# Self-attention in two transformer layers: the side steps of a head placed in steps 0 to 5 of its eight

## The chip, the core and the metric

The kernel runs on one core of a Trainium2 chip. The metric is the device time in microseconds (us) of one launch. The core has a matrix engine (TensorE, PE in the profile, with its weight loads as PEld), a vector engine (VectorE, DVE), an activation engine (ScalarE, ACT), GpSimd (POOL) and SyncE (SP), which here only issues DMAs. Each engine runs its own instruction list in order, and the lists meet at semaphores only.

## What is computed

Two sequences of 1024 tokens by 256 go through two layers, one after the other, which makes four rounds (sequence by layer). Each layer is self-attention, cross-attention to 77 context rows of 192, and a gated feed-forward part:

```python
x = x + attention(layer_norm(x, g1, b1), layer_norm(x, g1, b1), wq1, wk1, wv1, wo1, bo1)
x = x + attention(layer_norm(x, g2, b2), context, wq2, wk2, wv2, wo2, bo2)
x = x + geglu_ff(layer_norm(x, g3, b3), w_ff1, b_ff1, w_ff2, b_ff2)
```

Attention has 16 heads of 64: `q = x @ wq`, `k = ctx @ wk`, `v = ctx @ wv`, softmax of `q k^T / 8`, times v, times `wo`. Everything is float32 in the reference. The kernel splits a float32 operand into a high and a low float16 part and multiplies three times (high by high, high by low, low by high).

## The kernel before

The change touches the self-attention of each round only. There the 16 heads go in 8 pairs, a pair has two head units (head 0, then head 1), and a unit has eight steps, 0 to 7. One step of a head makes a 128x1024 tile of scores. Per step the program holds:

- **peaks**: two matmuls (L769) of single precision parts for the unit that comes next, each into one of two PSUM banks, and for each a `tensor_reduce` on DVE (L1299, "minima") that finds the row maxima. PE may write the bank again when DVE has read it. After the last peak of the next unit (step 6), DVE combines them (L1303), and at the start of step 7 PE transposes the result (L776, "shift"), DVE copies it (L1309), and SP moves it by DMA into a row of `qb`, which the first score of the next unit needs (L796).
- **score**: four matmuls (L789, L796), then two exponentials on ACT (L1120, L1121), one to float32 and one to float16.
- **low part**: the difference of the two, one step later: in steps 1, 3, 5 and 7 ("refine", of tiles 0, 2, 4 and 6) on DVE (L1314), in the others ("polish", tiles 1, 3, 5 and, in step 0 of the next unit, 7) on POOL (L636).
- **value**: 24 short matmuls (L814 to L818) for the tile of three steps ago. After tiles 3 and 7 DVE scales the sum ("gather", L1320 and L1322).
- **one side step or none**, on PE right in front of the score: q, k or v of the next pair (half of the tokens each, L688 to L690; q and k have 6 matmuls of 512 columns, v has 24 of 128), a merge (four transposes of the finished output of the pair before, L826), or a context part (ck, cm, cv: key, key times query weights, and value of the cross-attention). All use one PSUM bank, `work1`. ACT copies the high part out, in front of the exponentials of its step; DVE then takes the low part out ("take", placed between its two minima of that step), and only then may PE begin the next side step. The takes are L1258 (q, k), L1264 (v), L1270 (merge), L1274 (ck, two instructions), L1280 (cm), L1289 (cv, three instructions).
- **weights**: SP fetches them, POOL scales and splits them in three instructions ("split": L585, L586, L589). In head 0 the split W of a 128x1024 piece stands in step 3 (pairs 0 to 5). In head 1 the split S (next q, k, v weights, 128x768) stands in step 3 and the split C (context weights) in step 7. The split S waits until PE has finished every side step placed up to there, its own step 3 included.

In POOL's list the order is polish 7 (of the unit before), polish 1, the split of step 3, polish 3, polish 5, the split of step 7. A table of numbers in `self_unit` says which step a side step goes into; each engine walks the same list of steps and issues its own share of each.

Of the kernel before, what the change touches and what calls it, by code (L numbers as in the profile page):

```python
# [115 lines left out]
Step = collections.namedtuple("Step", "kind step par head ahead")  # L116
# [6 lines left out]
def take(step):  # L123

    return Step("take", (step.kind, step.step), step.par, step.head, step.ahead)
# [12 lines left out]
def queries(par, ahead):  # L138
    return [Step("q", b, par, 0, ahead) for b in range(BLKS)]


def key_blocks(par, ahead):
    return [Step("k", b, par, 0, ahead) for b in range(BLKS)]


def values(par, ahead):
    return [Step("v", b, par, 0, ahead) for b in range(2)]


def maxima(par, head):  # L150

    first = [Step("arrive", 0, par, 0, 0)] if head == 0 else []
    tiles = [[Step("max", (t, h), par, head, 0) for h in range(BLKS)] for t in range(TILES)]
    tiles[0] = first + tiles[0]
    tiles[-1] = tiles[-1] + [Step("combine", 0, par, head, 0)]
    return tiles


def low(s, par, head):

    return [Step("polish" if s in POLISHED else "refine", s, par, head, 0)]


def value(s, par, head):

    out = [Step("value", s, par, head, 0)]
    if s % KEY_STEPS == KEY_STEPS - 1:
        out.append(Step("gather", s // KEY_STEPS, par, head, 0))
    return out


def self_unit(pair, head):

    par, last, first = pair % 2, pair == PAIRS - 1, pair == 0
    nxt, behind = (((par, 1), (1 - par, 0)), ((1 - par, 0), (1 - par, 1)))[head]
    prv = (par, 0) if head == 1 else (1 - par, 1)
    before = head == 1 or not first
    after = (1 - head) if last else 2
    peaks_of = maxima(*nxt)[1:] if after else [[]] * (TILES - 1)
    peaks_of.append(maxima(*behind)[0] if after > 1 else [])  # L180
    placed = collections.defaultdict(list)
    if not last and head == 0:
        placed[0] = [Step("start", 0, 1 - par, 0, 1)]
        for at, step in zip((0, 1, 2, 4), queries(1 - par, 1) + key_blocks(1 - par, 1)):
            placed[at].append(step)
    elif not last:
        for at, step in zip((1, 3), values(1 - par, 1)):
            placed[at].append(step)
    if head == 1 and not first:
        for at, h in ((4, 0), (6, 1)):  # L190
            placed[at].append(Step("merge", h, 1 - par, 0, -1))
    if head == 0:
        placed[5].append(Step("ck", 0, par, 0, 0))
        placed[7].append(Step("cm", 0, par, 0, 0))
    else:
        placed[5].append(Step("cv", 0, par, 0, 0))
    loads = collections.defaultdict(list)
    if head == 0:
        if pair + 2 <= PAIRS:
            loads[1].append(Step("fetch", ("S", pair + 2), par, 0, 0))  # L200
        if pair < 6:
            loads[3].append(Step("split", ("W", pair), par, 0, 0))
        loads[6].append(Step("fetch", ("C", pair + 1), par, 0, 0))
    else:
        if pair + 2 <= PAIRS:
            loads[3].append(Step("split", ("S", pair + 2), par, 0, 0))
        loads[7].append(Step("split", ("C", pair + 1), par, 0, 0))
        if pair < 5:
            loads[7].append(Step("fetch", ("W", pair + 1), par, 0, 0))
    out = [Step("unit", 0, par, head, 0)]  # L210
    for s in range(TILES):
        peaks = [step for step in peaks_of[s] if step.kind == "max"]
        if s == TILES - 1 and after:
            out.append(Step("shift", 0, *nxt, 0))
        out += [step for step in peaks_of[s] if step.kind == "arrive"] + peaks[:1]
        out += placed[s]
        out.append(Step("score", s, par, head, 0))
        out += [take(step) for step in placed[s] if step.kind in HIGH]
        out += peaks[1:] + [step for step in peaks_of[s] if step.kind == "combine"]
        out += loads[s]  # L220
        if s >= 1:
            out += low(s - 1, par, head)
        elif before:
            out += low(TILES - 1, *prv)
        if s >= LAG:
            out += value(s - LAG, par, head)
        elif before:
            out += value(TILES - LAG + s, *prv)
    return out


def self_steps():

    out = [Step("start", 0, 0, 0, 0)]
    out += taken(queries(0, 0) + key_blocks(0, 0) + values(0, 0))
    out += [Step("split", ("S", 1), 0, 0, 0)]
    out += sum(maxima(0, 0), []) + [Step("shift", 0, 0, 0, 0)] + maxima(0, 1)[0]
    for pair in range(PAIRS):
        out += self_unit(pair, 0) + self_unit(pair, 1)
    par = (PAIRS - 1) % 2  # L240
    out += low(TILES - 1, par, 1)
    for s in range(TILES - LAG, TILES):
        out += value(s, par, 1)
    return out + taken([Step("merge", h, par, 0, 0) for h in range(BLKS)])
# [1338 lines left out]
```

How the kernel before makes its waits and increments, by code:

```python
        def hold(eng, sem_, value):  # L444
            eng.wait_ge(sem_, value)
            eng.sem_inc(held, 1)
# [10 lines left out]
            def fetch(g, kind, n):  # L458
                i, l = fetched[0], g % LAYERS
                fetched[0] += 1
                e = i % 2
                if kind == "W":
                    dest, source = raw[e][:, :], io["pieces"][l * PIECES + n, :, :]
                else:
                    dest, source = raw[e][:, 0:6 * P], io["pairs"][(2 * l + (kind == "C")) * PAIRS + n, :, :]
                if i >= 2:
                    sp.wait_ge(raw_used[e], i // 2)
                sp.dma_start(dest, source).then_inc(raw_loaded[e], 16)
# [4 lines left out]
                def spread(which, step):  # L474
                    hold(sp, a.work_free, pace.n("take") + 1 + HIGH_RING)
                    if step.ahead:
                        sp.wait_ge(a.scores_full, pace.pairs(2 * TILES) + (CREDIT - 4 * TILES))
                    for head in range(2):
                        mine, others = [slice(r, r + DH) for r in (head * DH, (1 - head) * DH)]
                        up, low = [part[mine, :] for part in staged["qk".index(which)]]
# [8 lines left out]
                def do(step, pair):  # L491
# [10 lines left out]
                    elif step.kind == "shift":  # L502
                        sp.wait_ge(a.peak_free, pace.n(*PEAK) + 1 + PEAK_RING)
                        row = DH if step.head == 0 else 0
# [339 lines left out]
            def turn(index, p):  # L845
                pe.wait_ge(norm_ready, index * TILES + 2 * (p + 1))
                if p >= 2:
```

## Time and profile before

| what | value |
|---|---|
| three runs | 2564.97 us median (2563.12 to 2571.7) |
| the profiled execution | 2564.95 us |
| its span, first to last instruction | 2563.2 us |
| self-attention of round 1, pairs 0 to 7 | about 57 to 427 us of the span |
| one pair, shift to shift | 45.55 us |
| a side step's share of PE: q or k, v, merge, cm, ck, cv | 1.3, 1.34, 0.43, 0.4, 0.2, 0.73 us |

PE, DVE and ACT run side by side, so a share of busy time does not say which of them sets the pace; the lists of waits and the order of time around one wait do. The pattern of a pair repeats through a round within hundredths of a microsecond, so one pair in the middle (pair 3 of round 1, its head 1 from 217 to 240 us) stands for the rest. Ends of matmuls are modelled; distances between starts are not, and a PE wait is best read from them: behind the second peak matmul of a step, with the 24 value matmuls in between, the next item starts 0.96 us later if nothing holds it.

### The profile page before, as it was taken

How to read it: one execution, taken by the hardware profiler on the slowest of the kernel's cores; microseconds unless marked ns; L12 is line 12 of the kernel's file. 1: busy time of each engine (PE TensorE's matmuls, PEld its weight loads, DVE VectorE, ACT ScalarE, POOL GpSimd, SP SyncE). 2: the span in 40 equal slices, each digit the busy share in tenths (PEclk: the TensorE clock that was granted, in tenths of full speed). 3: DMA queues.
4: the chain of work that ended last, by engine and by line, in shares of the span. 5: the costliest groups of instructions: out<-in, count | busy, mean ns of one | idle time of the engine just before them, and what ended most of it. 6: DMA issues, size and time to landing. Idle time of an engine off the chain costs nothing.

```text
span 2563.2 us, 59118 instructions
## 1 busy us (share of the span) xinstructions
PE 2234.4 (87%) x25392; PEld 1483.4 (58%) x25392; DVE 1760.3 (69%) x3148; ACT 1475.6 (58%) x1948; POOL 1165.7 (45%) x730
## 2 busy tenths in 40 slices
PE   4999998879699999878959999988797999998788
PEld 1566666565366666656525666665653666666565
DVE  6888884545588888454548888845456888885454
ACT  2887885324288888432327888853243888884232
POOL 3667663212176666321216666632122676652311
PEclk8999999889799999888969999999897999999889
DMA  3312210000131221000023122100002223110000
GB/s 80 84 47 73 65 45 18 9 9 15 32 84 47 76 63 45 18 9 10 15 64 79 52 69 70 45 18 9 10 15 49 66 55 84 47 33 18 18 1 17
DMA packets 52437, 106.62 MB, mean 42 GB/s; under 512 B 9552, under 2 KB 13648, under 8 KB 52176
## 3 DMA queue, kind: packets, MB, share of 16 engines
q1 hardware_dynamic: 52176, 102.84, 15.1%
q8 instruction: 200, 3.28, 0.5%
q14 instruction: 61, 0.50, 0.1%
HBM read 50.25 MB, written 2.10 MB: 20 GB/s over the span
## 4 chain that ended last, share of the span: by engine, by line
PE 62%; DVE 19%; ACT 11%; issue 4%; DMA 2%; POOL 1%; SPq 1%; POOLq 0%; DVEq 0%; ACTq 0%
PE scores L688 7%; PE scores L689 7%; PE scores L690 7%; PE work L769 6%; PE scores L796 6%; PE scores L789 6%; DVE minima L1299 6%; DVE prob L1314 3%; PE work L688 3%; PE work L690 3%; PE work L689 3%; ACT prob L1120 3%; PE work L818 3%; PE work L814 3%; PE work L816 3%
## 5 line engine op out<-in xcount | busy, mean ns | idle before, releaser
L636 POOL TENSOR_TENSOR prob<-prob 128x1024 f16<-128x1024 f32 x256 | 582.5, 2275 | 557.1 <-ACT prob L1121 546.4
L1299 DVE TENSOR_REDUCE minima<-work 128x1 f32<-128x512 f32 x1024 | 681.3, 683 | 52.5 <-PE work L769 36.2
L1120 ACT ACTIVATE prob<-scores 128x1024 f32<-128x1024 f32 x512 | 526.0, 1027 | 125.9 <-PE scores L796 109.1
L1121 ACT ACTIVATE prob<-scores 128x1024 f16<-128x1024 f32 x512 | 522.9, 1021 | 0.0
L814 PE MATMUL work<-vals,prob 128*128 128x65 f16 x4096 | 429.7, 193 | 15.4 <-POOL prob L636 13.3
L818 PE MATMUL work<-vals,prob 128*128 128x65 f16 x4096 | 430.3, 195 | 0.0
L816 PE MATMUL work<-vals,prob 128*128 128x64 f16 x4096 | 430.2, 193 | 0.0
L814 PEld LDWEIGHTS work<-vals,prob 128*128 128x128 f16 x4096 | 383.5, 99 | 77.9 <-POOL prob L636 15.1
L769 PE MATMUL work<-ka,qa 128*128 128x512 f16 x1024 | 401.8, 396 | 24.9 <-DMA kb<-staged_k 15.7
L816 PEld LDWEIGHTS work<-vals,prob 128*128 128x128 f16 x4096 | 380.5, 97 | 58.1
L818 PEld LDWEIGHTS work<-vals,prob 128*128 128x128 f16 x4096 | 381.0, 97 | 0.0
L1314 DVE TENSOR_TENSOR prob<-prob 128x1024 f16<-128x1024 f32 x256 | 340.9, 1332 | 18.6 <-ACT prob L1121 17.6
L789 PE MATMUL scores<-qa,ka 128*128 128x512 f16 x1024 | 306.3, 381 | 6.3 <-DVE staged_q L1258 6.0
L796 PE MATMUL scores<-qb,kb 128*128 128x512 f16 (+1 forms) x1024 | 306.6, 381 | 2.7 <-DMA qb<-shift_rows 2.5
L688 PE MATMUL scores<-wide,oT 128*128 128x256 f16 x768 | 213.6, 278 | 12.8 <-DVE prob L1496 7.1
L605 POOL TENSOR_TENSOR var_eps<-mean_var,eps 128x2 f32<-128x2 f32 x48 | 11.3, 236 | 464.7 <-DVE mean_var L1333 464.3
L689 PE MATMUL scores<-wide,oT 128*128 128x256 f16 x768 | 213.5, 278 | 0.0
L690 PE MATMUL scores<-wide,oT 128*128 128x256 f16 x768 | 213.2, 278 | 0.0
L1135 ACT ACTIVATE hT<-work,params 128x256 f16<-128x256 f32 x96 | 54.4, 566 | 233.3 <-PE work L852 220.1
L688 PE MATMUL scores<-hT,wide 128*128 128x512 f16 (+1 forms) x416 | 172.4, 414 | 4.5 <-DVE prob L1496 4.5
L796 PEld LDWEIGHTS scores<-qb,kb 128*128 128x128 f16 (+1 forms) x1024 | 99.9, 98 | 127.6 <-DMA qb<-shift_rows 8.4
L769 PEld LDWEIGHTS work<-ka,qa 128*128 128x128 f16 x1024 | 100.3, 98 | 125.8 <-DVE minima L1299 42.9
(166 smaller groups left out, 4593.4 us busy)
## 6 DMA issues: line engine op xcount, KB each, us to landing
qa<-staged_q SPq DMA_DIRECT2D x128, 128.0 KB, 2.4
ka<-staged_k SPq DMA_DIRECT2D x128, 128.0 KB, 2.4
raw_even<-in_pairs SPq DMA_DIRECT2D x32, 384.0 KB, 3.4
raw_odd<-in_pairs SPq DMA_DIRECT2D x32, 384.0 KB, 3.3
raw_odd<-in_pieces SPq DMA_DIRECT2D x20, 512.0 KB, 3.5
raw_even<-in_pieces SPq DMA_DIRECT2D x20, 512.0 KB, 3.7
qb<-staged_q SPq DMA_DIRECT2D x64, 128.0 KB, 2.4
kb<-staged_k SPq DMA_DIRECT2D x64, 128.0 KB, 2.4
```

Of the source, the lines that this page charges most:

```text
L636: pool.tensor_tensor(prob[1][:, slot, :], prob32[:, slot, :], prob[0][:, slot, :], ALU.subtract).then_inc(a.polished, 1)
L688: pe.matmul(out, left[0], right[0], start=first, stop=False)
L689: pe.matmul(out, left[0], right[1], start=False, stop=False)
L690: return pe.matmul(out, left[1], right[0], start=False, stop=last)
L769: pe.matmul(out[:, :], qa[par][head][:, t * P:(t + 1) * P], ka[par][head][:, h * BLK:(h + 1) * BLK], start=True, stop=True)\
L796: last = pe.matmul(out[:, at], kb[par][head][rows_, keys], qb[par][head][rows_, q], start=False, stop=True)
L814: pe.matmul(out, p_hi, v[:, DH:VW], start=(first and i == 0 and t == 0), stop=False, skip_group_check=True)
L816: pe.matmul(out[:, 0:DH], p_hi, v[:, 0:DH], start=False, stop=False, skip_group_check=True)
L818: last = pe.matmul(out, p_lo, v[:, DH:VW], start=False, stop=(k == TILES - 1), skip_group_check=True)
L1120: act.activation(prob32[:, n % RING, :], source, ACT.Exp)
L1121: act.activation(prob[0][:, n % RING, :], source, ACT.Exp)\
L1299: dve.tensor_reduce(minima[:, t, h:h + 1], out[:, :], AX.X, ALU.max, negate=True)\
```

## The change

Only the numbers in `self_unit` differ; two of the changed places, and the whole as a table:

```diff
     if head == 1 and not first:
-        for at, h in ((4, 0), (6, 1)):
+        for at, h in ((3, 0), (4, 1)):
             placed[at].append(Step("merge", h, 1 - par, 0, -1))
     if head == 0:
-        placed[5].append(Step("ck", 0, par, 0, 0))
-        placed[7].append(Step("cm", 0, par, 0, 0))
+        placed[4].append(Step("ck", 0, par, 0, 0))
+        placed[5].append(Step("cm", 0, par, 0, 0))
```

| step | 0 | 1 | 2 | 3 | 4 | 5 | 6 | 7 |
|---|---|---|---|---|---|---|---|---|
| head 0 before | q0 | q1 | k0 | - | k1 | ck | - | cm |
| head 0 now | q0 | q1 | k0 | k1 | ck | cm | - | - |
| head 1 before | - | v0 | - | v1 | m0 | cv | m1 | - |
| head 1 now | v0 | - | v1 | m0 | m1 | cv | - | - |

Pair 0 has no merges; pair 7 has no q, k and v. POOL's and SP's lists keep every row in its place; on PE, ACT and DVE a side step's rows move with its step. DVE's list in head 1 of a pair with merges, from the take of v1 on (`vals` is the v take, `oT` a merge take, `prob` a refine, `xv` the cv take, `minima` the maxima of one peak). Before:

```order
L1264 SCALAR_TENSOR_TENSOR vals<-work,vals 128x8x64
L1299 TENSOR_REDUCE minima<-work 128x1
L1314 TENSOR_TENSOR prob<-prob 128x1024
L1299 TENSOR_REDUCE minima<-work 128x1
L1270 TENSOR_TENSOR oT<-work,oT 128x512
L1299 TENSOR_REDUCE minima<-work 128x1 x2
L1289 SCALAR_TENSOR_TENSOR xv<-work,mask,xv 124x64 x3
L1299 TENSOR_REDUCE minima<-work 128x1
L1314 TENSOR_TENSOR prob<-prob 128x1024
L1299 TENSOR_REDUCE minima<-work 128x1
L1270 TENSOR_TENSOR oT<-work,oT 128x512
L1299 TENSOR_REDUCE minima<-work 128x1
```

And now:

```order
L1264 SCALAR_TENSOR_TENSOR vals<-work,vals 128x8x64
L1299 TENSOR_REDUCE minima<-work 128x1
L1320 RECIPROCAL inv<-work 128x4
L1322 TENSOR_TENSOR o_nat<-work,inv 128x4x64
L1299 TENSOR_REDUCE minima<-work 128x1
L1270 TENSOR_TENSOR oT<-work,oT 128x512
L1299 TENSOR_REDUCE minima<-work 128x1
L1314 TENSOR_TENSOR prob<-prob 128x1024
L1299 TENSOR_REDUCE minima<-work 128x1
L1270 TENSOR_TENSOR oT<-work,oT 128x512
L1299 TENSOR_REDUCE minima<-work 128x1 x2
L1289 SCALAR_TENSOR_TENSOR xv<-work,mask,xv 124x64 x3
```

The v1 take is one step earlier, so the gather of step 2 now follows it. The take of m0 stands in front of the first refine shown, where it stood behind it, and the take of m1 has left the last step before the combine for the step before cv.

DVE's list in head 0, from the refine of step 3 (before) or the take of k1 (now) on; `kd` is the ck take, `wide` the cm take. Before:

```order
L1314 TENSOR_TENSOR prob<-prob 128x1024
L1299 TENSOR_REDUCE minima<-work 128x1
L1258 SCALAR_TENSOR_TENSOR staged_k<-work,staged_k 128x512
L1299 TENSOR_REDUCE minima<-work 128x1 x2
L1274 SCALAR_TENSOR_TENSOR kd<-work,kd 64x77 x2
```

And now:

```order
L1258 SCALAR_TENSOR_TENSOR staged_k<-work,staged_k 128x512
L1299 TENSOR_REDUCE minima<-work 128x1
L1314 TENSOR_TENSOR prob<-prob 128x1024
L1299 TENSOR_REDUCE minima<-work 128x1
L1274 SCALAR_TENSOR_TENSOR kd<-work,kd 64x77 x2
L1299 TENSOR_REDUCE minima<-work 128x1 x2
L1280 SCALAR_TENSOR_TENSOR wide<-work,wide 128x2x154
```

The take of k1 now comes before that refine, not after it, and the take of cm follows that of ck in the next step.

## Rows read from the trace of the kernel before

**Rows 1.** The page, part 1: busy time, share of the span, instructions.

```profile
PE 2234.4 (87%) x25392; PEld 1483.4 (58%) x25392; DVE 1760.3 (69%) x3148; ACT 1475.6 (58%) x1948; POOL 1165.7 (45%) x730
```

**Rows 2.** Who waited for whom: us in total, times, longest us.

```profile
PE work L776 <- DVE shift L1303: 72.3, 64, 1.7
...
PEld scores L796 <- DMA qb<-shift_rows: 8.4, 13, 1.3
...
PE scores L796 <- DMA qb<-shift_rows: 2.5, 4, 0.8
```

**Rows 3.** PE in order of time: start, us, what, idle before. Head 1, pair 3.

```profile
228.85 0.22 PE L690 MATMUL work<-wpS,hT 128*128 128x128 f16 x1
...
229.77 0.38 PE L769 MATMUL work<-ka,qa 128*128 128x512 f16 x1
...
230.73 0.38 PE L769 MATMUL work<-ka,qa 128*128 128x512 f16 x1
230.95 0.60 PE L826 MATMUL work<-ident,o_nat 128*128 128x128 f32 x4
...
232.25 0.38 PE L769 MATMUL work<-ka,qa 128*128 128x512 f16 x1
...
239.66 0.22 PE L776 MATMUL work<-ident,shift 128*8 128x128 f16 x1 [1.04 <-DVE shift L1303]
```

**Rows 4.** ACT in order of time, the same stretch.

```profile
231.80 0.60 ACT L1091 ACTIVATE oT<-work 128x512 f16<-128x512 f32 x1
```

**Rows 5.** DVE in order of time, the same stretch.

```profile
230.35 0.68 DVE L1299 TENSOR_REDUCE minima<-work 128x1 f32<-128x512 f32 x1
230.95 1.22 DVE L1314 TENSOR_TENSOR prob<-prob 128x1024 f16<-128x1024 f32 x1
232.08 0.68 DVE L1299 TENSOR_REDUCE minima<-work 128x1 f32<-128x512 f32 x1
...
238.03 0.68 DVE L1270 TENSOR_TENSOR oT<-work,oT 128x512 f16<-128x512 f32 x1
```

**Rows 6.** POOL in order of time, the same stretch: the split S.

```profile
229.37 0.83 POOL L585 TENSOR_SCALAR wpS<-raw_odd 128x768 f16<-128x768 f32 x1 [0.68 <-PE work L690]
...
231.08 2.60 POOL L589 TENSOR_TENSOR wpS<-raw_odd,wpS 128x768 f16<-128x768 f32 x1
```

**Rows 7.** PE, DVE and POOL in order of time, pair 0, where no merge is placed.

```profile
102.64 0.22 PE L776 MATMUL work<-ident,shift 128*8 128x128 f16 x1 [0.88 <-DVE shift L1303]
...
104.76 1.64 POOL L589 TENSOR_TENSOR wpC<-raw_odd,wpC 128x768 f16<-128x768 f32 x1
...
104.91 2.58 DVE L1314 TENSOR_TENSOR prob<-prob 128x1024 f16<-128x1024 f32 x1
...
108.19 0.38 PE L769 MATMUL work<-ka,qa 128*128 128x512 f16 x1
108.74 0.39 PE L688 MATMUL work<-hT,wpS 128*128 128x512 f16 x1 [0.18 <-DVE staged_q L1258]
```

**Rows 8.** PE, ACT and POOL in order of time, head 0, pair 3.

```profile
217.26 0.22 PE L776 MATMUL work<-ident,shift 128*8 128x128 f16 x1 [1.17 <-DVE shift L1303]
...
212.75 0.47 ACT L1097 ACTIVATE kd<-work 64x77 f16<-64x77 f32 x2
...
208.50 3.13 POOL L589 TENSOR_TENSOR wide<-raw_even,wide 128x1024 f16<-128x1024 f32 x1
211.83 2.13 POOL L636 TENSOR_TENSOR prob<-prob 128x1024 f16<-128x1024 f32 x1 [0.19 <-issue]
```

**Rows 9.** DVE in order of time, the same stretch.

```profile
208.43 1.21 DVE L1314 TENSOR_TENSOR prob<-prob 128x1024 f16<-128x1024 f32 x1
...
213.25 0.49 DVE L1274 SCALAR_TENSOR_TENSOR kd<-work,kd 64x77 f16<-64x77 f32 x2 [0.47 <-ACT kd L1097]
213.76 0.69 DVE L1299 TENSOR_REDUCE minima<-work 128x1 f32<-128x512 f32 x1
214.49 1.22 DVE L1314 TENSOR_TENSOR prob<-prob 128x1024 f16<-128x1024 f32 x1
```

More of the change, by code:

```diff
@@ L183, in self_unit @@
         placed[0] = [Step("start", 0, 1 - par, 0, 1)]
-        for at, step in zip((0, 1, 2, 4), queries(1 - par, 1) + key_blocks(1 - par, 1)):
+        for at, step in zip((0, 1, 2, 3), queries(1 - par, 1) + key_blocks(1 - par, 1)):
             placed[at].append(step)
     elif not last:
-        for at, step in zip((1, 3), values(1 - par, 1)):
+        for at, step in zip((0, 2), values(1 - par, 1)):
             placed[at].append(step)
     if head == 1 and not first:
-        for at, h in ((4, 0), (6, 1)):
+        for at, h in ((3, 0), (4, 1)):
             placed[at].append(Step("merge", h, 1 - par, 0, -1))
     if head == 0:
-        placed[5].append(Step("ck", 0, par, 0, 0))
-        placed[7].append(Step("cm", 0, par, 0, 0))
+        placed[4].append(Step("ck", 0, par, 0, 0))
+        placed[5].append(Step("cm", 0, par, 0, 0))
     else:
```

## The prediction, made before the changed kernel ran

> **What bounds the kernel now.** I read four views, in this order. The page first: PE is busy for 87% of the span, DVE for 69% [rows 1], so PE sets the pace, and what can be won or lost is PE's waiting. Then the list of waits: in self-attention PE waits 64 times for the combine in front of the shift, 72.3 us in all, and a few times for the DMA of the shift row, 2.5 us by its matmuls and 8.4 us by its weight loads [rows 2]. Third the order of time on PE around one shift: it idles 1.17 us in head 0 [rows 8] and 1.04 us in head 1 [rows 3]; everywhere else in that pair the starts follow at their usual distances (0.96 us from a second peak to the next peak: 229.77 to 230.73 [rows 3]). Last, DVE and POOL side by side in that stretch, because the change moves DVE's instructions past refines while POOL's list stays.
>
> That last view shows what decides here. A refine (DVE) and a POOL instruction never make progress together. The refine of 230.95 takes 1.22 us and POOL's L589, begun 0.13 us after it, takes 2.60 us [rows 5, 6]; L589 of the same width (768) takes 1.64 us where it began first, and there the refine, begun 0.15 us after it, takes 2.58 us [rows 7]. So the second to start waits for the first: 1.08 us of refine are left when L589 ends (104.91 + 2.58 less 104.76 + 1.64), and L589 ends 1.5 us after a refine. Takes and minima, which read PSUM, show no such stretching.
>
> The Trainium skill says so too, in "SBUF — State Buffer", section Who interferes with whom: a DVE instruction with two SBUF inputs and a GpSimd instruction that reads SBUF contend, and whichever is first has the port pair for its whole length. The trace agrees (2.58 us against 1.22 us). By that rule every place where the change lets POOL be first is a loss; without it the sum is that of the second rival below.
>
> **Head 1, pairs 1 to 6: the refine of step 3.** I put the changed steps 2 and 3 (v1, then m0) on the clock of the steps that hold the same pair now (steps 3 and 4): v1's last matmul at 228.85, its second peak at 229.77, merge from 230.95 [rows 3].
> - POOL: the split S stands in step 3 and waits for PE's side step of that step, until now v1: L585 begins 0.52 us after v1's last matmul began (228.85 to 229.37) and L589 1.71 us behind it [rows 3, 6]. Now it waits for m0. Its fourth transpose begins at 231.27; a transpose takes 0.27 us where the v matmul takes 0.22, so L585 begins at 231.84 and L589 at 233.55. It lasts to 235.20.
> - DVE: ACT's copy of m0 runs 231.80 to 232.40 [rows 4]; the take follows at 232.43, the second minima 0.61 us later at 233.04 and the refine 0.60 us after that, at 233.64. (The gather now ends before, at 231.5, and the first minima at 232.1.)
> - So L589 is 0.09 us ahead; today it is 0.13 us behind [rows 5, 6]. The refine waits to 235.20 and ends at 236.28, 2.64 us instead of 1.22.
>
> What is late then, with 0.06 us from the end of a DVE instruction to PE's start: the next minima runs 236.20 to 236.88, and PE needs its bank for the first peak of step 5, due at 235.69: it starts at 236.94, **1.25 us** lost. The take of m1 ends at 237.48 and cv, due at 237.16, waits until 237.54: **0.38 us**. Behind cv the chain to the combine (ACT copy, three takes, minima, refine, two minima, combine) no longer holds the take of m1 in step 6 (0.60 us, 238.03 [rows 5]), nor PE the merge of 0.43 us: the shift idles 0.88 us, not 1.04, as it does in pair 0, where no merge stands there [rows 7, 3]: **-0.16 us**. And pair 0 shows what follows: polish 5 ends later against the shift, so the split C in step 7 begins its L589 just before the refine; that takes 2.58 us, and q1 of the next pair starts 0.55 us after its peak instead of 0.22 [rows 7]: **+0.33 us**. Sum 1.25 + 0.38 - 0.16 + 0.33 = 1.80 us per pair. A split S is in 6 pairs of rounds 1 to 3 and 5 of round 4: 23 x 1.80 = **+41.4 us**. The bounds of that term: if the refine is first, 0.20 (cv waits for m1's take) - 0.16 + 0.33 = 0.37 us, 8.5 us in all.
>
> **Head 1, pair 0.** v1 is in step 2 and the split S then waits for nothing but polish 1, which ends 0.95 us after the score of step 2; L589 begins 1.71 us later, at 2.7. The refine is due at 3.05. POOL is first by 0.3 us; the refine ends at 5.4, and the first peak of step 5, due at 5.02, starts at 6.06. Later waits are as now. 4 x 1.04 = **+4.2 us**.
>
> **Head 0, pairs 0 to 5 (24 units with a split W).** The split W starts behind polish 1, so L589 stays at 208.50 [rows 8]. Its refine was 0.07 us ahead (208.43 [rows 9]); k1 in step 3 (1.3 us of PE in front of the score) puts it at 209.88. L589 alone takes what a polish of that width takes, 2.13 us [rows 8], to 210.63; the refine ends at 211.71, 0.7 us late. On that clock (score of step 3 ended at 208.71): minima 211.63 to 212.31, so the first peak of step 5, due at 211.90, starts at 212.37 (0.47 lost); the take of ck, two instructions, ends at 212.72 and cm waits from 212.59 to 212.78 (0.19 lost). The minima behind it, the cm take at about 214.08 and then 0.40 + 0.60 + 1.13 + 0.60 + 0.71 + 0.32 us to the shift put it at 217.84, 0.84 us after PE could. That is 1.50 us in place of 1.31 (the 1.17 of the row, counted by starts), or 1.37 if the instruction lag behind the ck take vanishes (213.76 to 214.49 is 0.73 us where such a pair of rows is else 0.60 apart [rows 9]). I take +0.10 us: **+2.4 us**.
>
> **Head 0, pairs 6 and 7 (8 units, no split W).** Here the change works as drawn. cm in step 5 instead of ck: ACT's copy of ck starts 2.03 us after the score of step 4 and DVE's first take 0.50 us behind it [rows 8, 9]; cm's take is one instruction of 0.40 us for 0.51, and the lag of 0.13 goes, so the combine comes 0.22 us earlier while PE has 0.2 us more to do (cm 0.40, ck 0.20): 0.42 less waiting. 8 x 0.42 = **-3.4 us**.
>
> **The rest.** v0 in step 0 puts 1.34 us of PE in front of the score that needs the shift row, cm's 0.4 us leave: where that DMA was late in head 1, it is covered. The price lies between 2.5 and 8.4 us [rows 2]; by the starts I take **-3 us**. In pair 7 head 1 the exponentials pace the unit; m1's copy (0.60 us [rows 4], 0.48 start to start) now precedes the fifth, and polish 5, the split C and polish 7 behind it, on which the last values wait, come that much later: 3 x 0.4 = **+1.2 us** (round 4 has no such split). The matrix work, all ACT work and the DMAs are the same in number and size; the k parts are spread one step earlier, which nobody waits for.
>
> Sum: 41.4 + 4.2 + 2.4 - 3.4 - 3 + 1.2 = +42.8 us. Against the profiled execution, 2564.95 us (span 2563.2 and 1.75 around it, the median of the three runs within 0.02): **2608 us**, 1.7% slower.
>
> **Rivals.**
> - *The refine of step 3 stays first.* The lead of L589 is 0.09 us, and the trace shows the order at 0.15 ahead and at 0.13 behind, nothing between. If DVE wins such a start, the first term is 8.5 instead of 41.4: +9.9 us, 2575 us. For it: the lead hangs on two latencies I carried from v to a merge. Against: they repeat within 0.01 us in all pairs.
> - *The exclusion doesn't bite, and the chain before the shift is what counts.* Then each head 0 gains 0.42 us (32 x 0.42 = 13.4), head 1 is even (cv waits 0.20, the shift 0.16 less: 24 x 0.04 = +1), and with -3 + 1.2 it comes to -14 us, 2551 us. That is the gain the steps themselves promise: nothing beside the last peaks. Against it: two L589 would have to drift by 0.3 us and more (pair 0, and 24 times head 0, where the refine falls 1.4 us into L589).
> - *It only shifts waits.* A step's takes lean on ACT's copies and one PSUM bank; what the shift no longer waits, cv and cm wait. With the races half lost, half won by luck against gains elsewhere, it ends within 0.3% of now: 2565 us.
>
> **How the numbers follow.** Forecast 62%, first rival 18%, second 10%, third 10%. 0.3% is 7.7 us, about what a measurement of this kernel can tell from no change. Slower by more than that: the forecast and two thirds or more of the first rival (2575 with 5 us around it, the bound at 2572.7), 76%. Within: the third and the rest of the first, 14%. Faster: the second, 10%. The forecast's own range is 2600 to 2617 (23 x 0.2 for the head 1 term, 24 x 0.15 for head 0). The range reaches down over the first rival: 2568 to 2618.
>
> **What would show it.** In head 1 of a middle pair the refine of step 3 takes 2.6 us, not 1.2, with L589 begun 0.1 us before it and 1.64 us long; behind it the first peak of step 5 starts 2.2 us after the second of step 4, not 0.96. In head 0 of pairs 0 to 5 a refine takes 1.8 us inside L589. The waits for the combine fall from 72 us to about 55, those for minima rise by some 40. A q1 starts 0.33 us late in every pair, not only in pair 1. The forecast is wrong if the refine of step 3 keeps 1.2 us in pairs 1 to 6, or if PE waits in places that I have at nothing (value behind a polish).

## Result, and the profile after the change

The changed kernel takes 2607.54 us (median; 2606.72 to 2610.6) against 2567.97 (2563.12 to 2571.7) for the kernel before, four runs each: a ratio of 1.0157, 95% interval 1.0135 to 1.018. It is slower. The profiled execution took 2607.38 us, its span 2605.6, so 42.4 us more than that of before. (Every experiment below has runs of the kernel before beside it; their median lies between 2564.2 and 2568.0 us, so differences of one or two microseconds between medians of different sets say nothing.)

The page first, part 1 (busy time, share of the span, instructions) and part 4 (the chain that ended last):

```profile
span 2605.6 us, 59118 instructions
...
PE 2248.1 (86%) x25392; PEld 1483.9 (57%) x25392; DVE 1819.9 (70%) x3148; ACT 1476.7 (57%) x1948; POOL 1139.2 (44%) x730
...
PE 50%; DVE 32%; ACT 10%; issue 3%; DMA 2%; POOL 1%; SPq 1%; POOLq 0%; DVEq 0%; ACTq 0%
```

Part 4 of the page before:

```profile
PE 62%; DVE 19%; ACT 11%; issue 4%; DMA 2%; POOL 1%; SPq 1%; POOLq 0%; DVEq 0%; ACTq 0%
```

PE still makes up most of that chain, but DVE's part of it has grown from 19% to 32%.

No engine has an instruction more than before [rows 1], yet DVE is busy for 59.6 us longer and POOL for 26.5 us less. In part 5 of the two pages one group, the refines (line, engine, operation and tile, times | busy us, mean ns | idle before), grows by 64.6 us. Before:

```profile
L1314 DVE TENSOR_TENSOR prob<-prob 128x1024 f16<-128x1024 f32 x256 | 340.9, 1332 | 18.6 <-ACT prob L1121 17.6
```

After:

```profile
L1314 DVE TENSOR_TENSOR prob<-prob 128x1024 f16<-128x1024 f32 x256 | 405.5, 1584 | 18.7 <-ACT prob L1121 18.7
```

The same 256 instructions on the same data take 19% longer on average. Who waited for whom in the kernel after (us in total, times, longest us), the lines that answer to [rows 2]:

```profile
PE work L776 <- DVE shift L1303: 50.4, 64, 1.1
PE work L769 <- DVE minima L1299: 50.3, 87, 1.2
PE work L814 <- POOL prob L636: 16.1, 8, 4.6
...
PE work L688 <- DVE oT L1270: 4.7, 23, 0.2
PE work L688 <- DVE staged_q L1258: 4.2, 24, 0.2
PE scores L796 <- DMA qb<-shift_rows: 3.3, 2, 2.0
```

The combine is waited for 22 us less (72.3 before), the minima 41 us more: that line read

```profile
PE work L769 <- DVE minima L1299: 9.2, 36, 0.6
```

before. The two lines of L688 have 23 and 24 waits of 0.2 us, one per pair with such steps: cv waits for the take of m1, q1 for that of q0.

Where the wait for minima arises is seen in order of time (start, us, what, idle before). DVE in head 1 of pair 3, the stretch of [rows 5]:

```profile
238.11 0.69 DVE L1270 TENSOR_TENSOR oT<-work,oT 128x512 f16<-128x512 f32 x1 [0.25 <-ACT oT L1091]
238.72 0.68 DVE L1299 TENSOR_REDUCE minima<-work 128x1 f32<-128x512 f32 x1
239.31 2.62 DVE L1314 TENSOR_TENSOR prob<-prob 128x1024 f16<-128x1024 f32 x1
241.86 0.68 DVE L1299 TENSOR_REDUCE minima<-work 128x1 f32<-128x512 f32 x1
242.46 0.67 DVE L1270 TENSOR_TENSOR oT<-work,oT 128x512 f16<-128x512 f32 x1
```

POOL beside it, the stretch of [rows 6]:

```profile
237.50 0.83 POOL L585 TENSOR_SCALAR wpS<-raw_odd 128x768 f16<-128x768 f32 x1 [1.07 <-PE work L826]
...
239.21 1.64 POOL L589 TENSOR_TENSOR wpS<-raw_odd,wpS 128x768 f16<-128x768 f32 x1
```

And PE, the stretch of [rows 3]:

```profile
240.39 0.38 PE L769 MATMUL work<-ka,qa 128*128 128x512 f16 x1
...
242.59 0.39 PE L769 MATMUL work<-ka,qa 128*128 128x512 f16 x1 [1.08 <-DVE minima L1299]
243.19 0.27 PE L688 MATMUL work<-wpC,cT 128*124 128x128 f16 x1 [0.21 <-DVE oT L1270]
...
248.82 0.22 PE L776 MATMUL work<-ident,shift 128*8 128x128 f16 x1 [0.87 <-DVE shift L1303]
```

L589 of the split S starts 0.10 us ahead of the refine of step 3 and keeps its 1.64 us; the refine takes 2.62 us; the next minima ends at 242.54, and the first peak of step 5 starts 2.20 us after the second of step 4, not 0.96. Such a stretch stands in pairs 1 to 6 of rounds 1 to 3 and in pairs 1 to 5 of round 4, 23 times, and the refine takes 2.62 or 2.63 us in each. A middle pair, shift to shift, is 47.45 us long; it was 45.56.

### The profile page after: what moved, and what is told of

Same layout as the page of the kernel before. It is cut to its first block, busy times and chain, and to the rows that moved or that the text cites. A ratio compares the mean times of both kernels' runs of the same rounds, so it can differ in the third digit from the quotient of the medians.

```text
span 2605.6 us, 59118 instructions
## 1 busy us (share of the span) xinstructions
PE 2248.1 (86%) x25392; PEld 1483.9 (57%) x25392; DVE 1819.9 (70%) x3148; ACT 1476.7 (57%) x1948; POOL 1139.2 (44%) x730
## 4 chain that ended last, share of the span: by engine, by line
PE 50%; DVE 32%; ACT 10%; issue 3%; DMA 2%; POOL 1%; SPq 1%; POOLq 0%; DVEq 0%; ACTq 0%
DVE minima L1299 10%; DVE prob L1314 10%; PE scores L688 7%; PE scores L689 7%; PE scores L690 7%; PE work L769 4%; PE scores L796 4%; PE scores L789 4%; PE work L688 3%; PE work L690 3%; PE work L689 3%; ACT prob L1120 2%; ACT prob L1121 2%; PE work L818 1%; DVE hT L1346 1%
## 5 line engine op out<-in xcount | busy, mean ns | idle before, releaser
L636 POOL TENSOR_TENSOR prob<-prob 128x1024 f16<-128x1024 f32 x256 | 607.0, 2371 | 620.2 <-ACT prob L1121 607.9
L814 PE MATMUL work<-vals,prob 128*128 128x65 f16 x4096 | 430.9, 193 | 16.7 <-POOL prob L636 16.1
L1314 DVE TENSOR_TENSOR prob<-prob 128x1024 f16<-128x1024 f32 x256 | 405.5, 1584 | 18.7 <-ACT prob L1121 18.7
L688 PE MATMUL scores<-wide,oT 128*128 128x256 f16 x768 | 213.9, 278 | 12.7 <-DVE prob L1496 7.1
L688 PE MATMUL scores<-hT,wide 128*128 128x512 f16 (+1 forms) x416 | 172.0, 413 | 4.5 <-DVE prob L1496 4.5
```

The costliest lines, as they stand in the source:

```text
L636: pool.tensor_tensor(prob[1][:, slot, :], prob32[:, slot, :], prob[0][:, slot, :], ALU.subtract).then_inc(a.polished, 1)
L688: pe.matmul(out, left[0], right[0], start=first, stop=False)
L814: pe.matmul(out, p_hi, v[:, DH:VW], start=(first and i == 0 and t == 0), stop=False, skip_group_check=True)
L1314: dve.tensor_tensor(prob[1][:, slot, :], prob32[:, slot, :], prob[0][:, slot, :], ALU.subtract).then_inc(a.refined, 1)
```

## Experiments

Two theories were put against each other. **P, port order**: a refine (or a split's subtraction) that starts second waits until the other engine's instruction has ended, and the change lets POOL start first. **B, bunching**: side steps in neighbouring steps wait for one another's takes through the one bank `work1`, whatever POOL does. "Ahead" and "behind" are the start of L589 (or of the line that is L589 there) against the start of the refine. The diffs show the lines that matter, against the kernel named in front of each; where they use a tile `pause`, its allocation is left out.

### Each head alone

The change in head 1 alone:

```diff
-        for at, step in zip((1, 3), values(1 - par, 1)):
+        for at, step in zip((0, 2), values(1 - par, 1)):
-        for at, h in ((4, 0), (6, 1)):
+        for at, h in ((3, 0), (4, 1)):
```

> The kernel before with the new places in head 1 alone (v in steps 0 and 2, merges in 3 and 4); head 0 as before. Theory P (port order: L589 of the split S starts just before the refine of step 3, which then waits for it): the whole loss sits here, +41.4 (pairs 1 to 6) + 4.2 (pair 0) - 3 (shift row covered by v0) + 1.2 (end of the round), about +43 us over the kernel before; in a middle pair the refine of step 3 takes 2.6 us. Theory B (bunching: side steps in neighbouring steps wait for each other's take through the one bank, in both heads): the loss of 42 us is shared by the heads in proportion to the neighbouring side steps, so +15 to +25 us, and it shows as waits of side steps for takes, not as a long refine.

Measured: 2609.99 us (2608.89 to 2612.68) against 2564.19, ratio 1.0186 (1.0164 to 1.0207). In a middle pair, by starts on PE, the peak of step 5 is 1.24 us late, cv 0.38 and q1 0.33, and a pair lasts 47.28 us. The 46 us over the kernel before are what P expected (43); B's 15 to 25 are not. The row of the refine on DVE:

```profile
236.66 2.62 DVE L1314 TENSOR_TENSOR prob<-prob 128x1024 f16<-128x1024 f32 x1
```

The change in head 0 alone:

```diff
-        for at, step in zip((0, 1, 2, 4), queries(1 - par, 1) + key_blocks(1 - par, 1)):
+        for at, step in zip((0, 1, 2, 3), queries(1 - par, 1) + key_blocks(1 - par, 1)):
-        placed[5].append(Step("ck", 0, par, 0, 0))
-        placed[7].append(Step("cm", 0, par, 0, 0))
+        placed[4].append(Step("ck", 0, par, 0, 0))
+        placed[5].append(Step("cm", 0, par, 0, 0))
```

> The kernel before with the new places in head 0 alone (k1, ck, cm in steps 3, 4, 5); head 1 as before. Theory P: 24 x 0.10 - 8 x 0.42 = -1 us, within 3 us of the kernel before, with a refine of 1.8 us inside L589 of the split W in pairs 0 to 5 and one of 1.2 us in pairs 6 and 7. Theory B: +15 to +25 us.

Measured: 2570.56 us (2563.26 to 2577.86) against 2564.19, ratio 1.0029 (1.0016 to 1.0042), 6 us slower, where about nothing was expected. The refine in a split W takes 1.83 us, the peak behind it is 0.48 late, cm 0.18, the shift 0.82, as foreseen; but a pair is 0.16 us longer, not 0.10, and pair 0 has a loss of its own (below). Its profiled execution is 2.8 us longer than that of the kernel before; where the rest of the 6 us by the medians comes from is not shown. Head 1 holds nearly all of the loss.

### Nudging the order, changed kernel and kernel before

If only the order of two starts decides, a small delay on one engine is worth 30 us or more, with every side step in its place. In the changed kernel, an addition of two columns on POOL ahead of L589 of the split S:

```diff
+                if kind in "S" and splits[0] >= 2:
+                    pool.tensor_tensor(pause[:, :], eps[:, :], eps[:, :], ALU.add)
```

> The changed kernel with one POOL addition on 128x2 numbers (about 0.2 us, result unused) in front of each split S; nothing else moves. Theory P: L589 now starts some 0.1 us behind the refine of step 3 instead of 0.09 us ahead, the refine takes 1.2 us again and L589 2.6; pairs 1 to 6 lose 0.37 us instead of 1.80, so 33 us less than the changed kernel, about 2575 us; pair 0 (POOL 0.3 us ahead) stays as it is or gains part of 4 us. Theory B: no change from the changed kernel (2607 us), or 0.2 us per pair more.

Measured: 2612.3 us (2609.64 to 2617.46) against 2564.19, ratio 1.0194 (1.0173 to 1.0214). The delay didn't reach its size: the addition is shown with 0.19 us, but L589 moved by 0.05 us only, to 0.054 us ahead, and the refine waited still. So this run does not test the expectation of 33 us less; it narrows the border between the two orders. In the kernel before, six memsets of two columns on DVE ahead of the refine of step 3 in head 1:

```diff
+                        if head == 1 and s == 2:
+                            for k in range(6):
+                                dve.memset(pause[:, 2 * k:2 * k + 2], 0.0)
```

> The kernel before, no side step moved, with six memsets of 128x2 numbers on DVE (result unused, 0.05 to 0.1 us each) in front of the refine of step 3 in each head 1. Their own time is 0.3 to 0.6 us of DVE in a unit where DVE has slack. Theory P: the refine, so far 0.13 us ahead of L589 of the split S, now starts behind it and waits for it: DVE is 1.6 us late in 27 pairs, of which PE loses about 1.5 us each in front of the peak of step 5 and cv, so about +40 us over the kernel before, without any side step moved. Theory B: +0 to +5 us.

Measured: 2565.96 us (2561.08 to 2572.1) against 2564.19, ratio 1.001 (0.9997 to 1.0022). The six moved the refine by 0.06 us together; it started 0.067 us before L589 and kept 1.22 us. So this one does not test its expectation of 40 us either. What it shows is that a delay of the refine reaches PE in full: head 1, shift to shift, is 22.46 us long for 22.40. Both delays had to be larger. On POOL now an addition of 128 columns:

```diff
+                if kind in "S" and splits[0] >= 2:
+                    pool.tensor_tensor(pause[:, :], ident[:, :], ident[:, :], ALU.add)
```

> As pool_later, with an addition on 128x128 numbers in place of the one on 128x2, since that one put L589 only 0.05 us back (0.054 us ahead of the refine of step 3 where the changed kernel has 0.102) and the refine still took 2.67 us. From the rows of L636 (2.13 us for 1024 columns) about 0.3 us. Theory P: L589 starts 0.1 to 0.3 us behind the refine, the refine takes 1.2 us in pairs 1 to 6, PE gets back 1.43 us in each of 23: 33 us less than the changed kernel, that is about 9 to 12 us over the kernel before. Theory B: no change from the changed kernel.

Measured: 2581.02 us (2577.14 to 2585.05) against 2565.85, ratio 1.0075 (1.0046 to 1.0103): 26.5 us less than the changed kernel by the medians, 21 by the two ratios, for work that was added. DVE in head 1 of pair 3:

```profile
237.48 1.21 DVE L1317 TENSOR_TENSOR prob<-prob 128x1024 f16<-128x1024 f32 x1
```

POOL beside it (L590 is L589 there):

```profile
235.56 0.40 POOL L596 TENSOR_TENSOR pause<-ident 128x128 f16<-128x128 f32 x1 [0.96 <-PE work L829]
...
237.63 2.56 POOL L590 TENSOR_TENSOR wpS<-raw_odd,wpS 128x768 f16<-128x768 f32 x1
```

L590 starts 0.15 us behind, so now it waits (2.56 for 1.64 us) and the refine doesn't. The pair is 46.05 us long instead of 47.45, 1.40 us less, where 1.43 were expected. The whole falls short of the expected 33 us: it is 15 us over the kernel before, not 9 to 12. The stretches from the second shift of a round to its last give 30.7 us of it; the time outside them is 5.6 us longer in this execution than in that of the changed kernel, most of it in the first stretches of the rounds, where the granted clock differs from execution to execution. The counterpart in the kernel before, on DVE:

```diff
+                        if head == 1 and s == 2:
+                            for k in range(2):
+                                dve.tensor_reduce(pause[:, k:k + 1], ident[:, :], AX.X, ALU.max)
```

> The kernel before with two reductions of 128x128 numbers on DVE (results unused, about 0.15 us each) in front of the refine of step 3 in head 1, in place of the six memsets, which took 0.06 us together and left the refine 0.067 us ahead. Theory P: the refine now starts about 0.15 us behind L589 of the split S and takes 2.6 us; PE loses about 1.5 us in each of 27 pairs, about +40 us over the kernel before with no side step moved. Theory B: +0 to +5 us.

Measured: 2609.61 us (2606.68 to 2611.35) against 2565.85, ratio 1.0185 (1.0158 to 1.0212). DVE, the two reductions (0.47 us) and the refine:

```profile
237.57 0.47 DVE L1316 TENSOR_REDUCE pause<-ident 128x1 f32<-128x128 f32 x2
237.96 2.46 DVE L1318 TENSOR_TENSOR prob<-prob 128x1024 f16<-128x1024 f32 x1
```

POOL, 0.26 us ahead of it:

```profile
237.70 1.64 POOL L590 TENSOR_TENSOR wpS<-raw_odd,wpS 128x768 f16<-128x768 f32 x1
```

A pair is 1.63 us longer and the whole 44 us by the medians (about 40 expected), and no side step had moved. Not all of it is the order: the two reductions put the refine back by 0.39 us, and the six memsets had shown that such a delay reaches PE in full. The other 1.24 us of a pair, three quarters, are the refine's wait (2.46 us for 1.22). With the counterpart on POOL this leaves no room for B as the main cause: the same placing of side steps is 1.40 us a pair dearer or cheaper by the order of two starts, and the old placing has most of the loss as soon as POOL starts first.

### Holding the order by a semaphore

If POOL's L589 waits for the refine, the order is certain in both heads. In the changed kernel (the lines that hand `after` on to the split are left out):

```diff
+                if after is not None:
+                    pool.wait_ge(a.refined, after)
                 pool.tensor_tensor(low, source(e), high, ALU.subtract).then_inc(raw_used[e], 1)
...
+                            tile = 6 if kind == "C" else 2
+                            after = pace.lows(Step("refine", tile, *pace.unit, 0))
```

> The changed kernel with one more wait on POOL: L589 of the splits W, S and C starts only when the refine of its step (tile 2, 2 and 6) is done. Every refine then takes 1.2 us. Theory P: head 1 of pairs 1 to 6 loses 0.04 us instead of 1.80, pair 0 nothing, q1 is on time, and each head 0 gains 0.42 us: 14 us less than the kernel before, 55 us less than the changed one. Theory B: within 5 us of the changed kernel, since every side step stays where it is.

Measured: 2592.38 us (2589.16 to 2600.72) against 2565.85, ratio 1.0124 (1.0092 to 1.0156). A gain over the kernel before was expected, so this is a miss, and it has two parts. Head 1 is as foreseen (the refine of step 3 takes 1.22 us). But in head 0 the split W now ends later, so polish 3 starts later, and the refine of step 5 starts second to that. POOL in head 0 of pair 3 (L643 is the polish, and x2 merges polish 3 and polish 5):

```profile
213.50 2.13 POOL L591 TENSOR_TENSOR wide<-raw_even,wide 128x1024 f16<-128x1024 f32 x1 [2.83 <-DVE prob L1321]
215.83 5.19 POOL L643 TENSOR_TENSOR prob<-prob 128x1024 f16<-128x1024 f32 x2 [0.19 <-issue]
```

DVE beside it:

```profile
212.13 1.22 DVE L1321 TENSOR_TENSOR prob<-prob 128x1024 f16<-128x1024 f32 x1
...
216.76 2.27 DVE L1321 TENSOR_TENSOR prob<-prob 128x1024 f16<-128x1024 f32 x1
```

The combine comes later and the shift idles 1.67 us (1.17 before [rows 8]). Together a pair is 46.18 us long, 0.62 more than before. The second part is the clock. PE in stretches that hold one wait, and in what follows it (stretch, length, PE busy, matmuls in brackets, granted clock, DMA share, GB/s), first around the shift at 857.4, then around the one at 903.6 us; both waits are 1.67 us:

```profile
855.00:857.40 2.40, 0.74 (x24) 1.00 0.54 163
857.40:860.90 3.50, 3.48 (x52) 1.00 0.00 1
901.20:903.60 2.40, 0.74 (x24) 1.00 0.03 8
903.60:907.10 3.50, 3.50 (x26) 0.56 0.00 1
```

Behind the second, the granted clock is at the lower of its two levels (1.2 GHz of 2.4) for some 3.5 us: 26 matmuls instead of 52. That happened behind 11 of the 24 such waits in this execution, and each time the stretch to the next shift is 1.6 us longer (23.6 instead of 21.97 in the middle pairs): 11 x 1.6 = 18 of the 22.6 us that the self-attention is longer than in the kernel before. The kernel before and the changed one show full clock from the second shift of a round to its last; in the ones with head 1 alone and with the two reductions it fell twice, in the one with six memsets once, each time behind the shift of head 0 in pair 0, which waits 1.6 us there. So the order held by a semaphore moved the wait onto the chain before the shift, where PE idles in one piece, and the clock made it dearer.

Steps 5 and 6 freed of takes, on top of that, so that the refine of step 5 comes earlier:

```diff
-        for at, h in ((3, 0), (4, 1)):
+        for at, h in ((1, 0), (3, 1)):
...
-        placed[5].append(Step("cm", 0, par, 0, 0))
+        placed[7].append(Step("cm", 0, par, 0, 0))
...
-        placed[5].append(Step("cv", 0, par, 0, 0))
+        placed[4].append(Step("cv", 0, par, 0, 0))
```

> As ordered, with other places: head 0 q0 q1 k0 k1 ck - - cm, head 1 v0 m0 v1 m1 cv - - -, so that steps 5 and 6, the two in front of the shift, have none. Theory P with the chain read from the rows: without a take in step 5 the refine of step 5 waits for its exponentials only, and the shift comes about 0.77 us after PE could instead of 0.9 (head 0) and 1.04 (head 1): another 10 to 20 us less than ordered, 24 to 34 us less than the kernel before. If side steps in neighbouring steps do cost by themselves, it is no better than ordered.

Measured: 2610.48 us (2606.88 to 2617.25) against 2565.85, ratio 1.0198 (1.0164 to 1.0233), a miss again. The refine came earlier, and so it lies within the polish for longer. In head 0 of pair 3, POOL and then DVE beside it:

```profile
221.49 5.19 POOL L643 TENSOR_TENSOR prob<-prob 128x1024 f16<-128x1024 f32 x2 [0.19 <-issue]
```

```profile
222.03 2.67 DVE L1321 TENSOR_TENSOR prob<-prob 128x1024 f16<-128x1024 f32 x1
```

In head 1 the refine of step 5 meets polish 3 too. DVE in head 1 of pair 2:

```profile
198.33 2.04 DVE L1321 TENSOR_TENSOR prob<-prob 128x1024 f16<-128x1024 f32 x1
```

The shift then idles 1.45 us in head 1 (0.88 with the waits on the refine alone) and 1.67 in head 0, and where the clock does not fall a pair is 46.89 us long, 0.7 more than with those waits alone. In twelve stretches it did fall (mean 0.93 over the stretch). Both misses left polish 3 out of the reckoning: a split held back holds back the polishes behind it in POOL's list. They do not speak for B, since a refine of 2.0 to 2.7 us in front of the late shift is in the rows of both.

### Getting POOL out of the way instead

The split W need not stand early. Here it goes to step 7 of head 0, v1 to step 3, and the merges to steps 4 and 6 as before; the fetch of the split C's weights moves too, since the splits take their buffers in turn:

```diff
-        for at, step in zip((0, 2), values(1 - par, 1)):
+        for at, step in zip((0, 3), values(1 - par, 1)):
-        for at, h in ((3, 0), (4, 1)):
+        for at, h in ((4, 0), (6, 1)):
-            loads[3].append(Step("split", ("W", pair), par, 0, 0))
-        loads[6].append(Step("fetch", ("C", pair + 1), par, 0, 0))
+            loads[7].append(Step("split", ("W", pair), par, 0, 0))
     else:
+        loads[1].append(Step("fetch", ("C", pair + 1), par, 0, 0))
```

> Head 0 as in the change (k1, ck, cm in steps 3, 4, 5) but with the split W in step 7, behind polish 5, and the fetch of the context weights in step 1 of head 1, so that SP does not wait for it in front of the shift row; head 1 v0 and v1 in steps 0 and 3, merges in 4 and 6 as before. The waits on the refine of the run ordered had moved L589 out of the refine of step 3, but polish 3 then began late and the refine of step 5 fell into it (2.2 us in 24 units of head 0). Theory P: here no refine of steps 1, 3 and 5 meets a POOL instruction; each head 0 waits 0.42 us less than before (32 x 0.42 = 13.4), the shift row is covered by v0 (3 us): 16 us less than the kernel before, ratio 0.994. Theory B (neighbouring side steps cost by themselves): no gain over head0_alone (1.003).

Measured: 2547.5 us (2546.07 to 2549.61) against 2566.33, ratio 0.993 (0.9917 to 0.9944), faster than both kernels and as P expected (0.994). DVE in head 0 of pair 3, the refines of steps 5 and 7:

```profile
214.89 1.22 DVE L1314 TENSOR_TENSOR prob<-prob 128x1024 f16<-128x1024 f32 x1
...
219.92 1.32 DVE L1314 TENSOR_TENSOR prob<-prob 128x1024 f16<-128x1024 f32 x1
```

POOL, the split W in step 7, second now:

```profile
220.25 2.98 POOL L589 TENSOR_TENSOR wide<-raw_even,wide 128x1024 f16<-128x1024 f32 x1
```

PE, the shift that answers to the first of [rows 8]:

```profile
217.65 0.22 PE L776 MATMUL work<-ident,shift 128*8 128x128 f16 x1 [0.72 <-DVE shift L1303]
```

Its wait is 0.72 us (1.17 before), and a pair is 45.11 us long, 0.45 less. (The refine of step 7 is the first of the two and still takes 1.32 us: it begins before L586, the scaling in front of L589, has ended.) This is what the change's head 0 promises where nothing on POOL stands in it. The last one puts the merges into steps 1 and 2 as well, with the 128-column addition ahead of the split C's L589, so that this comes second to the refine of step 7:

```diff
-        for at, h in ((4, 0), (6, 1)):
+        for at, h in ((1, 0), (2, 1)):
...
+                if kind == "C" and splits[0] >= 2:
+                    pool.tensor_tensor(pause[:, :], ident[:, :], ident[:, :], ALU.add)
```

> As w_in_step_7, with the merges in steps 1 and 2 of head 1 (v0 m0 m1 v1 - cv - -) and a POOL addition on 128x128 numbers (0.26 us by pool_later_2) in front of each split C, so that its L589 starts behind the refine of step 7 instead of 0.15 us ahead. Theory P: the refine of step 3 stays 0.13 us ahead of L589 of the split S, the shift of head 1 idles 0.88 us instead of 1.04 (24 x 0.16 = 4 us), q1 is on time: 20 us less than the kernel before, ratio 0.992. Theory B: side steps now neighbour each other in all of steps 0 to 3 of head 1, so slower than w_in_step_7.

Measured: 2552.36 us (2547.45 to 2554.86) against 2566.33, ratio 0.9945 (0.993 to 0.996). The shift in head 1 idles 0.88 us, 0.16 less, as foreseen:

```profile
236.80 0.22 PE L779 MATMUL work<-ident,shift 128*8 128x128 f16 x1 [0.88 <-DVE shift L1306]
```

But v1, now one step behind m1, starts 0.25 us late, for m1's take. That is B, at its size in this placing: it exists, and it eats what the shift gained (45.18 us a pair). The expected 0.992 is missed, and the median is 4.9 us above that of the kernel with the split W in step 7 alone. Some 3 us of these stand at the ends of rounds 1 to 3: there PE waits 5.4 us for the last low parts (0.43 and 4.96), against 4.4 in that kernel (0.57 and 3.80).

## Why the prediction was right

**Mechanism and place.** The step on which it stood, that L589 of the split S comes 0.09 us ahead of the refine of step 3, measured 0.10 us, and the refine took 2.62 us for the 2.64 forecast. The port rule cited there (the Trainium skill, "SBUF — State Buffer", section Who interferes with whom) holds in all twelve profiled executions: in some 3000 places where a refine and a POOL instruction overlap, the one that started first keeps its usual time (unless it was itself second to one before), and the other ends later by what was left of the first. Alone, L589 of that width takes 1.64 us and the refine 1.22. The one-input scalings of a split (L585, L586) take part as well, which the prediction did not use. POOL in head 1 of pair 7 in the kernel before, where such a scaling takes 0.83 us when nothing holds it:

```profile
413.90 0.83 POOL L585 TENSOR_SCALAR wpC<-raw_odd 128x768 f16<-128x768 f32 x1
414.70 1.80 POOL L586 TENSOR_SCALAR raw_odd<-raw_odd 128x768 f32<-128x768 f32 x1
```

DVE beside it, second to L585 and first to L586:

```profile
414.08 1.72 DVE L1314 TENSOR_TENSOR prob<-prob 128x1024 f16<-128x1024 f32 x1 [0.60 <-ACT prob L1121]
```

The prediction says that takes and minima show no such stretching, and the traces agree: no minima of self-attention takes more than 0.70 us, beside a POOL instruction or not.

**Head 1, pairs 1 to 6.** Forecast 1.25 + 0.38 - 0.16 + 0.33 us; measured by starts 1.24, 0.38, -0.17 and 0.33. Every term is within 0.01 us; each was carried over from a row of the same pattern elsewhere in the trace: the late q1 and the shorter shift from pair 0 [rows 7], where the pattern already stood. One effect of 0.08 us was left out: before, the first peak of step 4 came that much late behind two minima in a row, and now it doesn't. So the stretches of head 1 lost 0.10 us less than forecast, 2.3 us over 23. q1 is late because of the split C, as forecast; DVE in step 7 of pair 3:

```profile
251.09 2.57 DVE L1314 TENSOR_TENSOR prob<-prob 128x1024 f16<-128x1024 f32 x1
```

**Head 1, pair 0.** Forecast 1.04 us; the peak of step 5 is 1.02 us late. From shift to shift, cm apart, it is 0.87 us, so the term was 0.7 us too high over four rounds.

**Head 0, pairs 1 to 5.** Peak, cm and shift were forecast at 0.47, 0.19 and 0.84 us and measured 0.48, 0.19 and 0.82. Their sum is 1.49, as written, against 1.31 before. The forecast left room for 1.37 in place of 1.50, if a lag behind the ck take vanished, and took 0.10 between the two differences (0.06 and 0.19). The lag stayed: a pair is 0.16 us longer. With the q1 a little later than carried over, that is 1.6 us over 20 units. (The refine there is 0.6 us late, not 0.7 as the prediction says; nothing else in it used that number.)

**Head 0, pairs 6 and 7.** In pair 6 the shift waits 0.45 us less (0.42 forecast). In pair 7 it waits 0.40 us less, but a peak in step 0 waits 0.97 us for minima where it waited 0.44: there the split C's race holds up the minima instead of a q1. The forecast had that race as a late q1, also in pair 7 of rounds 1 to 3, which has no q1. So pair 7 lost 0.19 us, where these two terms together gave a gain of 0.1 to 0.4: 1.4 us too low in all.

**A term that was missed.** In head 0 of pair 0, L589 is 0.5 us ahead of the refine, not 1.4; the refine takes 2.70 us and the peak is 1.35 us late, not 0.48. The forecast applied the numbers of the middle pairs to it. The first stretch of a round, shift to shift, shows it where the clock is equal (mean 0.93 in round 4 of both): 25.11 us against 23.85, 1.26 us, of which 0.4 is cm, which now stands before the second shift and no longer behind it: 0.86 us where 0.10 was forecast, some 3 us over four rounds. In the two profiled executions it is hidden: that stretch starts at the lower clock level, longest in two rounds of before (mean 0.77), and the four sum to 103.0 us in both.

**The shift row's DMA.** -3 us forecast. By the distances between shifts it measured -3.2: before, 10 of them are 0.1 to 0.9 us longer than the others of their kind, 3.6 us in all; after, three, 0.4 us in all. The list of waits (PE 3.3 us for 2.5, PEld 8.0 for 8.4) shows what the forecast left out: v0 covers the row in the pairs that have a v0, and PE's matmuls no longer wait for it there. But pair 7 has no side step in front of these scores, and its head 1 has now lost cm there. Both waits that are left stand in pair 7, 1.3 us in head 0 and 2.0 in head 1, the latter behind the last shift of its round and so outside these distances.

**The end of a round.** 3 x 0.4 us forecast, and right. Before, PE waited 0.58 us for a refine and 3.80 for POOL there; now 4.75 for POOL alone, 0.37 more in each of rounds 1 to 3. The prediction named waits of a value behind a polish as a sign of being wrong where it had them at nothing; all of PE's (16.1 us, 13.3 before) stand here, where it had put them.

**The sum.** The table has the 42.4 us of the two spans by place; cm, 0.4 us per round, moves from behind the last shift of a round into its first stretch.

| place | forecast | measured |
|---|---|---|
| second shift of a round to its last, late shift rows left out | 44.2 | 44.3 |
| late shift rows there | -3 | -3.2 |
| first stretches, cm included | 2.0 | 0.0 |
| outside, cm gone | -0.4 | 1.3 |
| sum | 42.8 | 42.4 |

That it lies within 0.4 us of the forecast is luck in part. In the first row, 3.0 us too high (head 1) stand against 3.0 too low (head 0 and pair 7). The first stretches would have cost 5.0 us (4 x 1.26) at equal clock. And the 1.3 us outside are no measure of the end of a round: between two rounds the distance changed by -4.8, 6.2 and -0.2 us. By the medians of all runs the difference is 39.6 us.

**Waits and rivals.** Forecast 72 to about 55 us for the combine, and +40 for minima: 50.4 and +41. The first rival needed DVE to win at 0.09 us, and the runs show POOL winning with 0.02 us. Its ground, that the trace before had nothing between 0.15 ahead and 0.13 behind, was a misreading: [rows 8] and [rows 9] have DVE first by 0.07 us. The second rival's 2551 us are borne out as the price of the steps alone in two parts, not as a whole: in head 1 the placing is even where the refine is first (21.97 us from shift to shift in the kernel with the 128-column addition, 22.40 with cm's 0.40 in the kernel before), and head 0 gains 0.45 us with the split W in step 7. The third didn't occur.

## What to carry to other kernels

Where DVE runs two-input instructions on SBUF beside POOL instructions that read SBUF, read their lists side by side and treat each pair of near starts as a race: who is second waits for the whole of the other's rest. In these traces the wait shows as a longer instruction and not as idle time, so compare the mean duration of a group across kernels. Moving a step on one engine moves it against a list that stayed; the cure that paid was to move POOL's work to where DVE's chain isn't urgent, while holding POOL by a semaphore pushed its later work onto the next urgent place. A wait in one piece on TensorE may cost its clock on top (1.6 us behind a wait of 1.67 here).

## What the hardware showed that was not expected

- The order is decided by starts that lie very close. POOL was first with 0.021 us (pair 0 of the kernel with the 128-column addition, the refine took 2.70 us), 0.054, 0.10, 0.15 and 0.26 us ahead; DVE was first with L589 0.067, 0.13, 0.15 and 0.33 us behind. In the twelve profiled executions there is no case in which the one that started second won.
- Tiny instructions are poor delays. An addition of 128x2 on POOL is shown with 0.19 us and moved the next instruction by 0.05; one of 128x128 is shown with 0.40 and moved the next by 0.26. Six memsets of 128x2 on DVE moved the next by 0.06 us in all.
- The granted clock fell behind some waits of 1.67 us and not behind others of the same length (11 of 24 in one execution), each time for some 3.5 us and at a price of 1.6 us. From the second shift of a round to its last, over all twelve profiled executions, it fell behind 28 of 65 waits of 1.64 to 1.67 us and behind none of 1.46 us or less. What decides is not shown by these runs.
